# Layer 0: the third part of the stacked score operands is fetched from ScalarE's queue instead of SyncE's

## What is computed

```python
q = X @ Wq.T + bq                       # 32 heads of 8 features
k = encoder_output @ Wk.T + bk          # 8 groups of 8 features, each shared by 4 heads
v = encoder_output @ Wv.T + bv
scores = jnp.einsum('bgrqd,bgkd->bgrqk', q, k) / jnp.sqrt(jnp.float32(HD))
scores = jnp.where(causal_mask[None, None, None, :, :], -jnp.inf, scores)
scores = jnp.where(padding_mask[:, None, None, None, :], -jnp.inf, scores)
w = jax.nn.softmax(scores, axis=-1)
out = jnp.einsum('bgrqk,bgkd->bgrqd', w, v)
...
return out @ Wo.T + bo
```

## Time and profile before

| | us |
|---|---|
| median of 3 runs (lowest, highest) | 1297.38 (1296.94, 1299.64) |
| the profiled execution | 1297.1 |
| its span, from the first to the last instruction | 1295.3 |
| PE busy | 1172.4 (91% of the span) |
| VectorE busy | 1059.1 (82%) |
| ScalarE busy | 908.2 (70%) |
| GpSimd busy | 748.6 (58%) |

### The profile page before, as it was taken

The page is one execution under the profiler, slowest core; times in us unless marked ns, Lnnn a source line. Parts: engine busy times, 40 slices in busy tenths (PEclk is TensorE's granted clock), DMA queues, the critical chain, the costliest instruction groups (busy, mean ns, idle before and its releaser), DMA issues. The chain is left out here.

```text
span 1295.3 us, 30618 instructions
## 1 busy us (share of the span) xinstructions
PE 1172.4 (91%) x8917; PEld 930.4 (72%) x8917; DVE 1059.1 (82%) x2479; ACT 908.2 (70%) x3605; POOL 748.6 (58%) x1099
## 2 busy tenths in 40 slices
PE   2599999988899999999999999998999999399992
PEld 2256655644588888888888888886887788279992
DVE  6479999988798888988888899897788887656664
ACT  1166666657899899989989988997888787123331
POOL 3457777776756655665665666565556786313331
PEclk9699999999899999999999999999999999689996
DMA  7444444442130202220220221122211000722325
GB/s 171 92 87 90 90 88 82 82 79 47 56 117 2 87 18 69 86 69 17 86 86 0 86 86 36 50 86 85 71 50 55 30 34 21 293 75 77 90 83 195
DMA packets 145817, 100.47 MB, mean 78 GB/s; under 512 B 68541, under 2 KB 139198, under 8 KB 145728
## 3 DMA queue, kind: packets, MB, share of 16 engines
q1 hardware_dynamic: 134592, 87.28, 26.1%
q0 software_dynamic: 3744, 8.45, 1.8%
q10 hardware_dynamic: 7392, 3.64, 1.0%
HBM read 58.42 MB, written 42.48 MB: 78 GB/s over the span
## 5 line engine op out<-in xcount | busy, mean ns | idle before, releaser
L1418 POOL TENSOR_TENSOR head_rstd<-head_rstd,minus_half 128x4 f32<-128x4 f32 x192 | 223.8, 1166 | 15.1
L1406 ACT ACTIVATE squares<-ps 128x128 bf16<-128x128 f32 x768 | 202.0, 285 | 43.1 <-PE ps L1369 35.8
L1369 PE MATMUL ps<-w_proj_in,xq 128*128 128x512 f16 (+1 forms) x1024 | 210.4, 328 | 6.0 <-ACT headsT L1442 5.4
L1498 POOL TENSOR_TENSOR prob<-prob,rinv 128x512 f32<-128x512 f32 x128 | 140.4, 1098 | 108.5 <-DVE rinv L1493 108.3
L1442 ACT ACTIVATE headsT<-ps,l_hln 128x256 f32<-128x256 f32 (+1 forms) x256 | 168.2, 691 | 30.1 <-PE ps L1433 30.1
L1485 ACT ACTIVATE prob<-ps,nmax 128x128 f32<-128x128 f32 x512 | 182.2, 391 | 10.0 <-DVE nmax L1476 8.5
L1406 ACT ACTIVATION_READ_ACCUMULATOR squares<-ps 128x1 f32 x768 | 165.5, 216 | 0.0
L1426 DVE TENSOR_TENSOR heads_n<-ps,head_rstd 128x512 f32<-128x512 f32 x192 | 131.4, 684 | 25.5 <-POOL head_rstd L1418 25.4
L1369 PEld LDWEIGHTS ps<-w_proj_in,xq 128*128 (+1 forms) x1024 | 100.1, 98 | 53.9 <-issue 9.1
L1469 PE MATMUL ps<-headsT 128*128 128x128 f32 x1024 | 136.6, 277 | 1.0 <-DVE probT L1514 0.4
L1416 POOL TENSOR_TENSOR head_rstd<-head_squares,l_head_eps 128x4 f32<-128x4 f32 x192 | 47.1, 246 | 153.0 <-ACT squares L1406 152.1
(11 more groups left out here) (302 smaller groups left out, 2772.3 us busy)
## 6 DMA issues: line engine op xcount, KB each, us to landing
slots<-blank_slot SPq DMA_DIRECT2D x12, 1554.0 KB, 8.5
halves<-half_made SPq DMA_DIRECT2D x32, 256.0 KB, 2.5
w_proj_in<-halves SPq DMA_DIRECT2D x16, 512.0 KB, 10.0
taken<-slots SPq DMA_DIRECT2D x23, 259.0 KB, 3.4
w_out_raw<-in_wprojT SPq DMA_DIRECT2D x8, 512.0 KB, 3.9
half_raw<-in_winT SPq DMA_DIRECT2D x16, 256.0 KB, 2.9
half_raw<-in_woutT SPq DMA_DIRECT2D x16, 256.0 KB, 3.1
q_stack<-q_parts SPq DMA_DIRECT2D x48, 64.0 KB
```

Source lines behind the costliest of these rows:

```text
L1369: last = e.matmul(out, xq[:, k, which, slot_at], weights(k, hl, c0, n), start=(k == 0 and hl == 0), stop=(k == KD - 1 and hl == 1))
L1406: last = e.activation(squares[:, 4 * n + h, :], A[n][:, h * HD1:(h + 1) * HD1], ACT.Square, scale=HD1**-0.5, accum_out=hss[:, 4 * n + h:4 ...
L1418: e.tensor_tensor(hr[:, four], hr[:, four], t["half"][:, four], ALU.pow).then_inc(g_r[n].sem, 1)
L1498: e.tensor_tensor(prob[:, kind, :, :], prob[:, kind, :, :], spread(rinv[:, kind, :], P), ALU.mult).then_inc(g_p[kind].sem, 1)
```

## The change

The loop over the three parts is cut in two. Piece INS on SyncE issues parts 0 and 1 (10 transfers). A new piece INA on ScalarE has the two waits of INS and issues part 2 (5 transfers). It stands behind P2a in ScalarE's string. `MIXED` is a new table for all five engines.

```diff
     "scalar": (
-        "EX:5 P2a+++ F2a- EX:6 EX:7 P3h+++ OC:1 EX:0+ EX:1+ F4a- EX:2+ F4s- OTa WH++ F7a-- EX:3+ NTh++ EX:4+ "
-        "OC:0+"
+        "EX:5 P2a+++ INA++ F2a- EX:6 EX:7 P3h+++ OC:1 EX:0+ EX:1+ F4a- EX:2+ F4s- OTa WH++ F7a-- EX:3+ NTh++ "
+        "EX:4+ OC:0+"
     ),
...
+    def block_rows(e, i, p, n, q, k):
+        e.dma_start(qs[n * GP:(n + 1) * GP, p, :, :], q_parts[q].rearrange("(g f) t -> f g t", f=GP)).then_inc(d_ins.sem, 16)
+        for r in range(R0):
+            e.dma_start(kb[n * GP + r * HD0:n * GP + (r + 1) * HD0, p, :, r, :], of_group(k)).then_inc(d_ins.sem, 16)
+
     @s.piece("INS", "sync")
     def _(e, i, p):
         e.wait_ge(d_out.sem, d_out.at(i))
         e.wait_ge(pe_S.sem, pe_S.at(i - 2))
-        for n, (q, k) in enumerate(parts):
-            e.dma_start(qs[n * GP:(n + 1) * GP, p, :, :], q_parts[q].rearrange("(g f) t -> f g t", f=GP)).then_inc(d_ins.sem, 16)
-            for r in range(R0):
-                e.dma_start(kb[n * GP + r * HD0:n * GP + (r + 1) * HD0, p, :, r, :], of_group(k)).then_inc(d_ins.sem, 16)
+        for n, (q, k) in enumerate(parts[0:2]):
+            block_rows(e, i, p, n, q, k)
+
+    @s.piece("INA", "scalar")
+    def _(e, i, p):
+        e.wait_ge(d_out.sem, d_out.at(i))
+        e.wait_ge(pe_S.sem, pe_S.at(i - 2))
+        block_rows(e, i, p, 2, *parts[2])
...
 MIXED = {
...
-    "sync": "aaaaaaaaaaaaabaccccbccbcc",
+    "sync": "aaaaaaaaaabaaacacccbcccbcc",
```

More of the change, by code:

```diff
@@ L2040 @@
     "tensor": (
-        "aaaaaaaaaaaaaaaaaaaaaaaaaaaaaaaabaaaaaaaaaabaaaaaaaaaaaaaaaaaaabaaaaaaaaaaabbaaaaabaaababaaabbababab"
-        "ababbbbabababbbbababbbbbbbbbbbbbbbbbbbbbbbbbbbbbbbbbbbb"
+        "aaaaaaaaaaaaaaaaaaaaaaaaaaaaaaaaaabaaaaaaaabaaaaaaaaaaaaaaaaabaabaaaaaaabaaaabaaaaabbaabaabbaaabaabb"
+        "abaabbbababbabbbbaabbbbbbbbbbbbbbbbbbbbbbbbbbbbbbbbbbbb"
     ),
     "vector": (
-        "aaaaaaaaaaaaaaaaaabbaaaaaaaaaaaaaabaaabaaaaaaaabaaaaabbbabbbaaaabaababbacbaaacaabbbabbbbbcbcbabbabbb"
-        "abbbbbbbbcbbbbbbbbcbbbbbbbbbbbbbbbbcbbbbbbbbbbbcbbbbbbb"
+        "baaaaaaaaaaaaaaaaaaabaaaaaaaaaaaaaaabaabaaaaaaabaaaababbbabbaaabbaababacabcbbaaabaabbbabbbcbbabcabbb"
+        "babbbbcbbbbbbbbbcbbbbbbbbbbcbbbbbbbbbcbbbbbbbbbbbbbbbbb"
     ),
     "scalar": (
-        "aaaaaaaaaaaaaaaaaaaaaaaaaaaaaaaaabbbaaaabaaabaaabaabaabbaabcaaaabaabababaababccbbbacbbbbabababbbccbb"
-        "babbbbbbbbbbcbbbbbbbbcbbbbbb"
-    ),
-    "gpsimd": "aaaaaaaaaaaabaaaaaaaaaaabaaaaaaabbaababababaababaabbbabbabbbbbbbbbbbbbbbbbbbbbbbb",
-    "sync": "aaaaaaaaaaaaabaccccbccbcc",
+        "aaaaaaaaaaaaaaaaaaaaaaaaaaaaaaaaaaabaaabaabaabbbaaaababababaabbaaacaaabcbbababaaabbbbacbbbcaaabbbbbc"
+        "bbcabbbbbbbbbcbbbbbcbbbbbbbbbb"
+    ),
+    "gpsimd": "aaaaaaaaaaaaaaabaaaaaaaaabaaabaaababababbaabaabaababbabbabbbbbbbbbbbbbbbbbbbbbbbb",
+    "sync": "aaaaaaaaaabaaacaccbcccbcc",
 }
```

## The result

The changed kernel takes 1303.45 us (median of 20 runs, 1298.74 to 1307.69), the kernel before 1297.73 (20 runs, 1295.52 to 1301.47): ratio 1.0041, 95% interval 1.0028 to 1.0053. It is slower by some 5.7 us, where no change was forecast. The profiled execution of after took 1305.03 us, its span is 1303.3; that of before was 1295.3.

What follows compares the result with a forecast made beforehand. It took a 16.65 us loop through PE, POOL and VectorE, without SP or ACT, to set the even turn. Terms 0 - 0.3 - 1.5 + 0.4 + 1.1 + 0 = -0.3 us gave 1297.1 us against 1297.38; range 1292.8 to 1301.3.

Steps and rivals of the forecast that it cites:

- The rest of the new mix: Where the two layers mix, single layer 1 steps move by a few places: 0 us, bounds -2 and +2.
- The moved constants: 19 small VectorE operations stand ahead of another row maximum; PE waits 4.9 us there: +1.1 us, bounds -2.9 to +1.1.
- rival 4: ScalarE's queue sets S:0 in the even turns, issuing 2.25 us a part, +6 us over 10 turns: 1303, chance 0.10.
- The start: First S:0 comes earlier because SyncE's last issue ends 2.05 us earlier: gain of 1.5 us, from 0 to 2.05.
- Batch 1: Its part is issued behind 22 other issues on ScalarE, so S:0 may be late: +0.4 us, from 0 to 1.5.
- The even part: Layer 0 from 100 to 280 us: ScalarE's added issues cost 0, batch 4 gains 0.3 us, turns stay 16.7 to 17.3.
- The sum: Whole kernel: 0 - 0.3 - 1.5 + 0.4 + 1.1 + 0 = -0.3 us.
- Rival 5: Moved constants and mix each cost up to their bound, and the start gains nothing: 1300.9, chance 0.10.

Runs made afterwards that it cites:

- The order alone: Kernel before with the changed kernel's mix order, but SyncE fetching all three parts and the 19 constants in their old place: 1301.28 us, ratio 1.0023.
- the mix alone: Kernel before with the changed kernel's `MIXED` table, constants moved too, but SyncE still fetching all three parts: 1303.08 us, ratio 1.0038.
- the run with the rows later: Old mix, ScalarE fetching part 2 for batches 0 to 13, x load issued behind SyncE's two parts of batch 0: 1297.49 us, ratio 0.9988.
- fetch alone: Changed kernel with the old `MIXED` plus two INA letters for batches 14 and 15 in ScalarE's string: 1300.11 us against 1297.98, ratio 1.0018.

## Why the prediction was wrong

- **The rest of the new mix** is the first step that failed ("I take 0, bounds -2 and +2"). The order alone costs 3.4 us by its median and 3.0 by the ruler, over the bound, though its interval (1.2 to 4.7) reaches below it. This and the next term together were forecast at +1.1, at most +3.1; the mix alone measures 5.1 us, 3.1 to 6.9. Which moved step of layer 1 does it stays open; what is seen is PE waiting where it had not, 1.29 us for an exponential, 0.63 for `o_rows`, 0.46 for `xq`, and 0.9 us more at S:6 of batch 14. A bound cannot be had from the idle time that is there (13 us) and one slow stretch; it needs the waits that a step meets at its new place.
- **The moved constants** were mis-sized: +1.1, and +1.1 was also the upper bound. Alone they measure +3.7 (median; 1.2 to 4.3 by the interval) and +3.1 (ruler). I took their length from the old place, 4.2 us; at the new one they take 5.1 us, and begin behind 1.50 us in which VectorE waits for nothing that the profile shows. That PE waits there in one piece was right (5.83 us, 4.9 forecast), and so was the lower clock behind it (0.64 over the 5.8 us from 274.40 on).
- **Batches 14 and 15** were left out. I priced the fetch from an even turn (P2a + 3.15) and asked for rivals only there. In the written-out end ScalarE issues later beside the projection (270.10 - 263.94 = 6.2 us, against 250.85 - 246.41 = 4.4 in the turn before) and the landing takes 2.9 us, not 1.38. Behind the old mix this costs 2.4 us. It is near what rival 4 described (the issue takes 2.2 us there, rival 4's 2.25), at two turns and not at ten. In after itself waits of 0.70 and 1.72 us are left, but after is only 0.4 us slower than the mix alone: it is not what made after slow.
- **The start**: 1.5 us forecast, some 0.3 got. With SyncE's fetch the first S:0 starts at 34.08 to 34.81 in eight profiled runs (mean 34.50), with ScalarE's at 33.83 to 34.54 in six (34.18). The run with the rows later shows the cause, the DMA engines full of x (S:0 at 29.10). The Trainium skill, "DMA: Bandwidth & Descriptors", section "Issuing engines are not separate DMA queues", which I set against my term, was right: a second issuer saved issue time only.
- **Batch 1** of +0.4 can't be told from the spread. Its S:0 is 0.8 us later in the pair (58.14 against 57.33), and 0.5 us in the mean of four profiled runs with ScalarE's fetch and five without; but it waits for the part in after alone, for 0.21 us.
- **The even part** was right: from W of batch 2 to W of batch 11 turns of 16.70 to 17.54 us, each within 0.03 us of its old length, and no wait for ScalarE's part. Batch 4's wait is gone; the turn with it takes 16.72 and not 17.47 us, a gain of 0.75 where I took 0.3. That turn is 16.72 to 16.75 us in the four runs with ScalarE's fetch, and 16.73 to 19.51 in five that have SyncE's and the same first part, so the gain is anything from 0 to 2.8. S:0 of batch 2 waits 0.64 us for the part and starts 3.19 us behind P2a, where I had 3.15. That this fits is luck: the issue begins 0.67 us before P2a (see the last section), and issue and landing take 3.86 us.
- **The sum** should have had 3.7 (constants) and 3.4 (order), and 2.4 for the late fetch (1300.11 less 1297.68), less what these hide of each other; measured together they are 5.7. No rival stands as written. Rival 4's 1303 is the nearest number, by luck, since its ten late turns did not come. Rival 5, that constants and mix cost more, has the right cause and comes out 2.6 us too low.

## What to carry to other kernels

Price a change in a hand-written order also where the loop ends: the steady turn hides what the last turns show, since their neighbours, issue times and transfers are others. An edit of a whole order table is no small print; count what stands ahead of each wait at its new place, and give it a wide bound. And where a transfer changes its queue, look first for what stands in its way there: with ScalarE's start loads spread the same fetch gave some 5 us, and the loads alone 4.4.

## What the runs showed of the hardware that I had not expected

ScalarE issued transfers ahead of its own earlier work. INA stands behind P2a in the program, yet its issue begins 1.07 us before P2a does (timeline of ACT, fetch alone):

```profile
250.85 0.32 ACTq L686 DMA_DIRECT2D q_stack<-q_parts  x1
...
251.92 0.39 ACT L617 ACTIVATE xnT<-ps 128x256 f32<-128x256 f32 x1
...
251.95 0.72 ACTq L688 DMA_DIRECT2D k_blocks<-k_parts  x2
```

The issues also run beside exponentials, so in the even part they delay ScalarE less than my 1.75 us. A wait of 1.93 us of PE cost 3.03: the clock behind it was 0.57 for 4 us, and 1.00 in the 4 us after that. But one of 2.31 us cost 1.68, and after's 1.72 us cost nothing, so a wait's length doesn't give its price. And a VectorE step of 0.29 us took 1.60 us when it started 0.03 us behind a step of GpSimd.
